# An adaLN attention and mixture-of-experts block: a new end of the last expert, two gaps in on-chip memory, and a DRAIN of GpSimd

## The reference

```python
h = layernorm(x) * (1 + ca) + sa
q, k, v = split(h @ w_qkv)                  # 16 heads of 64
q = softmax(q * 64**-0.5, over the 64); k = softmax(k, over the 4096 rows)
x = x + ga * (einsum(q^T k per head, v) @ w_out + b_out)
h = layernorm(x) * (1 + cb) + sb
p = softmax(h @ Wg + bg)                    # 8 experts, the best 2 for each row
y = sum over the 2 of  p_e/sum * (gelu(h @ W1[e] + b1[e]) @ W2[e] + b2[e])   # 256 -> 1024 -> 256
x = x + gb * y
```

## Time and profile before

| | |
|---|---|
| median of three runs | 808.34 us (806.94 to 809.1) |
| the profiled execution | 809.0 us, its span 807.2 us |
| mean granted TensorE clock in the span | 0.97 |
| TensorE busy | 756.8 us, 94% of the span |
| VectorE, ScalarE, GpSimd busy | 608.3, 464.0, 340.1 us |

### The profile page before, as it was taken

One profiled execution on the slowest core, in us unless ns is written; L12 is line 12 of the kernel. 1 busy time (PEld: TensorE's weight loads), 2 busy tenths in 40 slices (PEclk: granted clock), 3 DMA queues, 4 the chain that ended last, 5 costly groups with the idle time before them and its releaser, 6 DMA issues.

```text
span 807.2 us, 16811 instructions
## 1 busy us (share of the span) xinstructions
PE 756.8 (94%) x5848; PEld 689.0 (85%) x5848; DVE 608.3 (75%) x1329; ACT 464.0 (57%) x841; POOL 340.1 (42%) x292
## 2 busy tenths in 40 slices
PE   5889999999999999975799999999999999999992
PEld 4767778788888789962799999999999999999992
DVE  6899999988898755799566768676676777776652
ACT  4465555756654532267647466666565766766461
POOL 2441413323322102300265655656555555656553
PEclk9999999999999999975799999999999999999997
DMA  7500000000000135670253532626244253333332
GB/s 283 169 1 1 1 1 2 1 2 2 1 1 2 53 106 177 200 189 6 93 158 54 152 59 48 164 44 164 58 107 105 41 134 77 47 47 60 60 47 40
DMA packets 45650, 59.71 MB, mean 74 GB/s; under 512 B 8018, under 2 KB 38804, under 8 KB 45460
## 3 DMA queue, kind: packets, MB, share of 16 engines
q0 software_dynamic: 14400, 21.98, 15.0%
q1 hardware_dynamic: 31188, 36.93, 14.2%
HBM read 40.63 MB, written 18.27 MB: 73 GB/s over the span
## 4 chain that ended last, share of the span: by engine, by line
PE 77%; DVE 13%; issue 5%; ACT 2%; POOL 1%; DMA 1%; SPq 0%; DVEq 0%; POOLq 0%; ACTq 0%
PE ps L1723 24%; PE ps L1737 23%; PE ps L1523 7%; PE ps L1481 6%; PE ps L1620 3%; PE ps L1548 3%; PE ps L1697 2%; PE ps L1532 2%; DVE q_max L958 2%; DVE q_sum L965 2%; DVE k_blk L1068 2%; PE ps L1640 2%; ACT at_lo L806 1%; DVE q_exp L959 1%; PE ps L1630 1%
## 5 line engine op out<-in xcount | busy, mean ns | idle before, releaser
L871 ACT ACTIVATE hid<-ps,b_col 128x256 f32<-128x256 f32 (+1 forms) x232 | 106.1, 509 | 113.5 <-PE ps L1723 109.3
L1737 PE MATMUL ps<-w_hi,hid_hi 128*128 128x256 f32 x544 | 153.6, 282 | 0.0
L1737 PE MATMUL ps<-w_lo,hid_hi 128*128 128x256 f32 x544 | 151.3, 278 | 0.0
L1737 PE MATMUL ps<-w_hi,hid_lo 128*128 128x256 f32 x544 | 151.3, 278 | 0.0
L1402 DVE TENSOR_TENSOR hid_lo<-hid,hid_hi 128x512 fp32r<-128x512 f32 (+1 forms) x116 | 90.9, 784 | 75.0 <-ACT hid_hi L875 74.5
L1723 PE MATMUL ps<-xT_hi,w_hi 128*128 128x256 f32 (+1 forms) x464 | 140.6, 303 | 1.6 <-DVE xT_lo L1356 1.6
L1723 PE MATMUL ps<-xT_hi,w_lo 128*128 128x256 f32 (+1 forms) x464 | 140.3, 302 | 0.0
L1723 PE MATMUL ps<-xT_lo,w_hi 128*128 128x256 f32 (+1 forms) x464 | 140.3, 302 | 0.0
L619 POOL DMA_INDIRECT out<-y,y_id x68 | 117.4, 1727 | 40.1 <-POOL y_id L614 17.6
L543 POOL TENSOR_TENSOR q_n<-q_exp,q_rec 128x1024 f32<-128x1024 f32 (+1 forms) x33 | 61.1, 1853 | 172.5 <-DVE q_rec L966 172.5
L607 POOL DMA_INDIRECT listed<-xrows,gid x87 | 95.6, 1098 | 42.3 <-POOL gid L603 24.6
(11 more groups left out here) (215 smaller groups left out, 1460.7 us busy)
## 6 DMA issues: line engine op xcount, KB each, us to landing
w_raw<-in_L_ffn_W SPq DMA_DIRECT2D x16, 1024.0 KB
x_all<-in_L_attn_x SPq DMA_DIRECT2D x8, 512.0 KB, 9.3
out<-x_all SPq DMA_DIRECT2D x8, 512.0 KB, 3.0
xrows<-x_all SPq DMA_DIRECT2D x8, 512.0 KB, 4.4
listed<-xrows,gid POOLq DMA_INDIRECT x87
out<-y,y_id POOLq DMA_INDIRECT x68, 4.0
wqk_raw<-in_L_attn_w_qkv SPq DMA_DIRECT2D x2, 512.0 KB, 6.2
wqk_raw<-in_L_attn_w_qkv SPq DMA_DIRECT2D x1, 1024.0 KB, 10.5
```

Source lines behind the costliest of these rows:

```text
L871: ins = act.activation(hid[:, m, 0:T], src, ACT.Gelu_apprx_tanh, bias=b1_col[:, e, m:m + 1])
L1737: last = pe.matmul(ps[:, bank, 0:D], a, w_, start=m == 0 and st, stop=m == M - 1 and sp_)
```

## The change

There are three parts. Two unused tensors are allocated: `h_gap`, 128 bytes in each partition, in front of `h_q`, so that `h_q` and what is allocated behind it in the first half lie 128 bytes further; and `x_gap`, 64 bytes, in front of `xT_full`, so that `xT_full`, `xT_hi`, `xT_lo` and `y` lie 64 bytes further. The last expert's blocks handle as many units of "the next block" as the block itself has, its narrow block copies `y_id` before it gathers and transposes after 6 instead of 18 matmuls of `second`, and the last wait for landings is VectorE's. GpSimd gets a DRAIN between the wide and the narrow loop of the last expert.

```diff
+        h_gap = sb("h_gap", [P, 32], F32, a_stack)
         h_q = sb("h_q", [P, HB, 2, C, STOK], F32R, a_stack)
...
+        x_gap = sb("x_gap", [P, 16], F32, c_stack)
         xT_full = sb("xT_full", [P, C, BT], F32, c_stack)
...
-            def gather(col, n):
+            def gather(col, n, units=BI):
...
-                for i in range(BI):
+                for i in range(units):
                     pool.indirect_dma_start(listed[:, i, :], None, xrows[:, :],
                                             bass.IndirectOffsetOnAxis(ap=gid[:, i:i + 1], axis=0)).then_inc(s_rows, 16)
-            def scatter(col, gv, size):
+            def rows_of(col, gv, size):
                 pool.wait_ge(s_added, now(pool, u) * 16 + DMA3)
                 pool.sem_inc(s_turn_pool, 1)
                 pool.tensor_copy(y_id[:, 0:size], ids[:, bass.ds(col, size)]).then_inc(s_yid, 1)
                 pool.wait_ge(s_yid, gv + 1)
+            def scatter(gv, size):
                 for i in range(size):
...
+                if last:
+                    pool.drain()
                 with pool.Fori(0, two) as b:
                     gv = now(pool, g)
-                    gather(ahead(three + b + 2), gv + 2)
-                    scatter(pool.snap(to, min_val=0, max_val=E * COLS - 2), gv, 2)
+                    if last:
+                        rows_of(pool.snap(to, min_val=0, max_val=E * COLS - 2), gv, 2)
+                        gather(ahead(three + b + 2), gv + 2, 2)
+                    else:
+                        gather(ahead(three + b + 2), gv + 2)
+                        rows_of(pool.snap(to, min_val=0, max_val=E * COLS - 2), gv, 2)
+                    scatter(gv, 2)
...
             experts(pool, numbers, expert)
-            pool.wait_ge(s_added, now(pool, u) * 16 + DMA3)
-            pool.wait_ge(s_rows, now(pool, g) * 48 + DMA3)
-            pool.sem_inc(s_done, 1)
...
-            def block_full(n):
+            def block_full(n, units):
...
-                    act.activation(xT_full[:, c, :], ps[:, XTB + c, 0:BT], ACT.Identity,
+                    act.activation(xT_full[:, c, 0:units * P], ps[:, XTB + c, 0:units * P], ACT.Identity,
...
-            def block_parts(n):
+            def block_parts(n, units):
+                r = slice(0, units * P)
...
-                    link(dve.tensor_copy(xT_hi[:, c, :], xT_full[:, c, :]))
-                    last = dve.tensor_tensor(xT_lo[:, c, :], xT_full[:, c, :], xT_hi[:, c, :].bitcast(F32), ALU.subtract)
+                    link(dve.tensor_copy(xT_hi[:, c, r], xT_full[:, c, r]))
+                    last = dve.tensor_tensor(xT_lo[:, c, r], xT_full[:, c, r], xT_hi[:, c, r].bitcast(F32), ALU.subtract)
...
-            def take(n):
-                dve.wait_ge(s_rows, n * 48)
+            def take(n, units):
+                dve.wait_ge(s_rows, now(dve, got) * 16)
                 dve.tensor_copy(y_next[:, :, :], listed[:, :, D:D + E]).then_inc(s_meta, 1)
                 normalize(0)
-                normalize(1).then_inc(s_norm, 1)
+                normalize(1).then_inc(s_norm, 1 + BI - units)
...
-                        if k == 3:
+                        if k == 3 and units == BI:
                             take_third()
...
             experts(dve, numbers, expert)
+            dve.wait_ge(s_added, now(dve, u) * 16 + DMA3)
+            dve.wait_ge(s_rows, now(dve, got) * 16)
+            dve.sem_inc(s_done, 1)
...
                 with pe.Fori(0, two) as b:
                     first(gv, 2)
-                    second(gv, 2, 0, most)
-                    block_T(gv + 1)
-                    second(gv, 2, 1, most)
-                    second(gv, 2, 0, end)
-                    second(gv, 2, 1, end)
+                    if last_expert:
+                        second(gv, 2, 0, range(0, 2))
+                        block_T(gv + 1, 2)
+                        second(gv, 2, 0, range(2, M))
+                        second(gv, 2, 1, range(0, M))
+                    else:
+                        second(gv, 2, 0, most)
+                        block_T(gv + 1)
+                        second(gv, 2, 1, most)
+                        second(gv, 2, 0, end)
+                        second(gv, 2, 1, end)
```

More of the change, by code:

```diff
@@ L644, in expert @@
                     gather(ahead(b + 2), gv + 2)
-                    scatter(pool.snap(to, min_val=0, max_val=E * COLS - 3), gv, 3)
+                    rows_of(pool.snap(to, min_val=0, max_val=E * COLS - 3), gv, 3)
+                    scatter(gv, 3)
                     pool.reg_add(to, to, 3)
                     pool.reg_add(g, g, 1)
+                if last:
+                    pool.drain()
                 with pool.Fori(0, two) as b:
                     gv = now(pool, g)
-                    gather(ahead(three + b + 2), gv + 2)
-                    scatter(pool.snap(to, min_val=0, max_val=E * COLS - 2), gv, 2)
+                    if last:
[5 more added lines that the diff above has]
+                    scatter(gv, 2)
                     pool.reg_add(to, to, 2)
@@ L880, in rows_block @@
                         act.reg_add(w, w, 1)
-                    block_full(gv + 1)
+                    block_full(gv + 1, size if last else BI)
                     act.reg_add(g, g, 1)
@@ L1323, in _ @@
             g = block_counter(dve, "g_dve")
+            got = block_counter(dve, "got_dve")
             chain.enter(dve.alloc_register("dve_chain"))
-            def block_parts(n):
+            def block_parts(n, units):
+                r = slice(0, units * P)
                 for c in range(C):
                     dve.wait_ge(s_bfull, n * C + ((BI - 1) * C + c + 1))
-                    link(dve.tensor_copy(xT_hi[:, c, :], xT_full[:, c, :]))
-                    last = dve.tensor_tensor(xT_lo[:, c, :], xT_full[:, c, :], xT_hi[:, c, :].bitcast(F32), ALU.subtract)
+                    link(dve.tensor_copy(xT_hi[:, c, r], xT_full[:, c, r]))
+                    last = dve.tensor_tensor(xT_lo[:, c, r], xT_full[:, c, r], xT_hi[:, c, r].bitcast(F32), ALU.subtract)
                 last.then_inc(s_blo, 1)
@@ L1373, in _ @@
             narrow_u = block_counter(dve, "narrow_u_dve")
+            dve.reg_add(got, got, BI)
             def expert(e, par, three, two, last_expert):
@@ L1386, in rows_block @@
                     T = size * P
+                    units = size if last_expert else BI
                     chain.begin()
@@ L1396, in rows_block @@
                         if k == 2:
-                            take(gv + 1)
-                        if k == 3:
+                            take(gv + 1, units)
+                        if k == 3 and units == BI:
                             take_third()
@@ L1405, in rows_block @@
                         w_low_part(2)
-                    block_parts(gv + 1)
+                    block_parts(gv + 1, units)
                     dve.wait_ge(s_added, now(dve, wide_u if size == 3 else narrow_u) * 16 + DMA3)
@@ L1424, in rows_block @@
                     dve.reg_add(u, u, size)
+                    dve.reg_add(got, got, units)
                     dve.reg_mov(wide_u if size == 3 else narrow_u, u)
@@ L1688, in _, with block_T @@
             g = block_counter(pe, "g_pe")
-            def block_T(n):
+            def block_T(n, units=BI):
                 pe.wait_ge(s_norm, n * 2 + (BI - 1))
-                for i in range(BI):
+                for i in range(units):
                     if i == 2:
```

## The result

The changed kernel takes 803.14 us (801.62 to 803.3, five runs) against 808.83 us before (806.94 to 809.6): a ratio of 0.9932, interval 0.9921 to 0.9943, a gain of 5.5 us. I had forecast 794. The profiled execution took 801.6 us with a span of 799.5. Two later executions of the kernel before took 1,079 and 4,044 us; they are in no ratio of this document.

A forecast was written before the change was run, and what follows sets the result against it. TensorE was taken to bound the experts' half and 160 to 290 us, GpSimd the end. From 808.3 us, gains of 5.1 (end), 7.0 (transposed rows) and 2.5 (split h) gave 793.7, stated as 794; range 790 to 804, about 0.8.

The forecast's parts named there:

- The gap before the transposed rows: Experts' half: 64 bytes more shorten each L1723 matmul by up to 6.3 ns, 7.0 us together; bounds nothing and 9.3.
- I price it at L1737's surcharge: L1723 would get L1737's distances, 320 and 64, and so its 7.0 ns above streaming time instead of 13.3.
- a floor of unknown origin: L1737 itself takes about 118 ns in some streams, so something else was taken to hold the pace there.
- the 3.0 us of the wide blocks: Part of the transposed rows' gain: 10 wide blocks x 48 matmuls x 6.3 ns.
- The gap before split h: First half, keys and queries: 128 bytes more were to gain 2.5 us; bounds 2.5 us either way.
- the 5.9 that I took: Nanoseconds each key or query matmul was to lose with distances of 256, priced from L1723 at 256 and 384 columns.
- The Trainium skill's rule: TensorE has two independent SBUF read ports, so loading weights steals no read bandwidth; by it both gaps are worth nothing.
- the rival beside that rule: Neither gap matters, only the end gains: 803.2 us, or 806.1 with two full DRAINs; chance 0.20.
- The end: Behind the last expert's wide block: new DRAIN, short closing DRAIN and moved wait gain 5.1 us; bounds 2.2 and 5.1.
- the closing DRAIN was to take well under 1 us: Sign to look for at the kernel's end: GpSimd's last DRAIN, 5.22 us before, becomes short.
- Two full DRAINs: Rival: both the new and the closing DRAIN cost full price, the rest as forecast: 797 us; chance 0.16.
- The slower case: Rival: the transposed rows' new place is worse, 9.3 us added, 812.5 us; chance 0.06.

The follow-up runs named there:

- e5: TensorE alone, not the block's computation: streams of 48 matmuls, operand distance stepped; at 256 columns 119.8 ns at 0 bytes, 117.9 at 64.
- e10: TensorE alone, one expert block's order of streams, first stream at distance 0, 64 or 128 bytes: the same 30 matmuls take 3.53 or 3.41 us.
- e9: The kernel before with only the 64-byte gap in front of the transposed rows: 807.19 us, ratio 0.9989.
- e12: The kernel before with only the 128-byte gap in front of split h: 807.88 us, ratio 0.9994.
- e6: GpSimd alone, not the block's computation: groups of 1 to 160 indirect DMAs, then a DRAIN; 82 ns for each further DMA up to 64.
- e3: The changed kernel without the DRAIN between the last expert's loops: 803.05 us, ratio 0.9933.
- e8: The changed kernel without its new DRAIN and with the last wait for the additions back on GpSimd: 804.80 us, ratio 0.9960.
- e7: The changed kernel with the DRAIN moved in front of the last expert's wide loop: 800.79 us, ratio 0.9908.

## Why the prediction was wrong

**The gap before the transposed rows: this term failed,** 7.0 us forecast, 1.3 found. The step was "I price it at L1737's surcharge". Two things were wrong in it. First, 113.7 ns is not the price of a distance of 64 bytes: alone on TensorE such a stream takes 117.9, against 119.8 at 0 (e5), and 113.7 is a second pace that the same stream at the same addresses may have or not have (e10). I had seen both paces at one distance in the earlier trace rows, 118.3 and 113.7, and called the higher one a floor of unknown origin instead of a second price for my term. Second, the gain in one stream is paid for by the next. In the narrow blocks before, behind a `first` at 120.0, the 18 of `second` ran at 113.4 in 10 of 19 and the 30 in 18 of 19. With the gap (e9), the 18 never do, and the 30 in 10 of 19, although no address of `second` has changed. `first` in narrow blocks goes from 120.0 to 116.6 ns on the mean (start to start, 893 spacings), 3.0 us; the 18 in front of the transposes go from 116.3 to 117.8 (476 spacings, 28 blocks of both kinds) and the 30 from 113.6 to 115.4 (532), 1.7 us back. The difference is the 1.3 us. And the 3.0 us of the wide blocks do not exist: 8.32 us before and after, and 0.4 ns of difference by distance at 384 columns in e5. What decides a stream's pace at its entry stays open.

**The gap before split h:** 2.5 us forecast, none found (e12). The distance from 128 to 0 is worth 5.4 ns in plain streams of 512 columns (e5), near the 5.9 that I took. In the kernel it does not come out so: from 160 to 290 us keys lose 1.7 ns and queries gain 2.2, and 206 x 1.7 - 162 x 2.2 is zero. Keys lose 4.9 (232.9 to 228.0) from 100 to 160, where VectorE is busy for 55.9 of 60 us and TensorE's time counts for little. The term was wrong by size; why keys and queries in their real order behave so was not tried.

**The Trainium skill's rule.** Its page "TensorE: Matmul & The Clock Gate", section "Step-by-step: what each phase is for", has the two operands read without cost to each other. The time measured, 803.14, is nearly the one that I had worked out for the rival beside that rule (803.2). That it is so near is luck: the kernel before now had 808.83 and not 808.3, the end gave 4.5 and not 5.1, and the gaps 1.3 and not nothing. The rule is not confirmed: the time of a matmul follows the distance of its operands by 2 to 6 ns, repeated at 256 bytes (e5). Whether the two disturb each other's reads, no run shows. I also made too much of the section "Back-to-back issue gap": it gives N/2.4 + 2.5 ns for a single matmul alone and not for a stream with a weight load each, so 113.7 and 120.0 against 109 said little.

**The end: right.** 5.1 us forecast, 4.5 measured. That the span before ended with GpSimd's own 5.2 us, that this price belongs to the DMAs issued since the last DRAIN (e6), that it is paid once wherever the DRAIN stands in the last expert (e3), and that the moved wait lets the landing run beside it (e8): all as worked out. The missing 0.6 us come from steps that I left out: GpSimd starts y_id 0.5 us behind the end of the DRAIN and the gid copy 0.79 behind y_id, a wait and restart like the 0.85 before the gathers. Against them the DRAIN was over 4.8 us behind the last wide addition and not 5.2, and the first gather took 1.03 and not 1.33. So the last addition starts 0.5 us later than forecast, counted from the last block's first matmul. One sign was wrong: the closing DRAIN was to take well under 1 us, and it lasted 2.3 us behind the last addition's issue, until the landing (e6). That cost nothing, since VectorE waited for the same landing. The new DRAIN did what was forecast of it and gained nothing by itself (e3); its place was the wrong one, since 4.3 us lie free one loop earlier (e7).

**The rivals.** Two full DRAINs did not come. The slower case, rows moved the wrong way, has no ground: at 256 columns all distances lie between 117.7 and 119.8 ns.

## What to carry to other kernels

Read what a closing GpSimd DRAIN costs before touching an end: in this kernel it was work piled up over the indirect DMAs, and a DRAIN in a place where GpSimd waits anyway takes it off the end for nothing. Put the last wait for landings on an engine that has nothing left to close. Two streams that differ in pace differ in more than the one thing that one has noticed: when a pace has two values at the same setting, a change of the setting is worth no more than a run of that stream alone shows, and the stream behind it belongs to the sum.

## What the runs showed of the hardware

- A GpSimd DRAIN costs 0.126 us with one indirect DMA since the last DRAIN and 82 ns more for each further one up to 64 (5.26 us), also when all has landed; 3.89 us at 160 (e6, one execution).
- A DRAIN behind few DMAs that are under way ends 0.1 to 0.2 us after the last landing (e6: 225.75 and 225.67; changed kernel: 799.17 and 798.96). A DRAIN with much piled up runs beside the landing and ends later (e3: 803.28 and 800.26).
- Float32r matmuls with a new stationary operand of 128 columns each depend on the distance of the two operands, with a period of 256 bytes: 117.7 to 119.8 ns at 256 columns, 173.3 to 175.8 at 384, 226.9 to 233.3 at 512 (e5, one execution).
- At a distance of 64 bytes and 256 columns there are two steady paces, 113 to 114 and 118 ns, and a stream of 30 keeps the one in which it began (e10, one execution; before, e9).
